# The second normalization's inverse root in a PSUM bank: two dependent steps a round in place of three

## What is computed

```python
x = x + tanh(g_xattn) * xattn(layernorm(x), ctx)      # window attention, 8 heads, 16 keys
x = x + tanh(g_ffn) * ffn(layernorm(x))
def layernorm(x, eps=1e-5):
    return (x - mean(x)) / sqrt(var(x) + eps)         # over the 2048 positions of a channel
def ffn(h):
    logits = einsum('th,eh->te', h, router_weight) + router_bias
    topk_w, topk_idx = top_k(softmax(logits), 8)
    w_dense = zeros.at[tokens, topk_idx].add(topk_w)
    return h * topk_w.sum(-1) + einsum('te,eh->th', w_dense, expert_bias)
```

## Time and profile before

| what | value |
|---|---|
| median of 3 runs | 1548.85 us (1548.09 to 1548.88) |
| profiled execution | 1549.06 us, span in the trace 1547.0 us |
| mean granted TensorE clock | 0.974 of full speed |
| TensorE busy | 1457.9 us (94%) |
| VectorE, ScalarE, GpSimd busy | 1232.8, 1156.2, 1160.6 us |

### The profile page before, as it was taken

How to read it: one execution, slowest core, us unless ns; L and a number is a source line. 1 busy time by engine, 2 the same in 40 slices (tenths; PEclk the granted TensorE clock), 3 DMA queues, 4 the chain that set the end, 5 groups by cost and what they waited for, 6 DMA issues and landing times.

```text
span 1547.0 us, 66674 instructions
## 1 busy us (share of the span) xinstructions
PE 1457.9 (94%) x28162; PEld 1196.4 (77%) x28162; DVE 1232.8 (80%) x2938; ACT 1156.2 (75%) x2025; POOL 1160.6 (75%) x1126
## 2 busy tenths in 40 slices
PE   4799999999999999999999999999999999999986
PEld 3577877878887888888788888878888887778764
DVE  5477887878888787888888788888878888787774
ACT  3588877778787877888787787878778787767652
POOL 4587777788777878778787887878788787677661
PEclk9799999999999999999999999999999999999896
DMA  7454455554545555454555545455554545434232
GB/s 231 122 127 107 127 149 140 145 161 113 162 131 140 144 154 162 112 161 133 140 144 154 162 114 162 131 140 147 152 161 114 160 133 140 123 82 134 57 77 90
DMA packets 365576, 210.39 MB, mean 136 GB/s; under 512 B 294496, under 2 KB 295520, under 8 KB 361056
## 3 DMA queue, kind: packets, MB, share of 16 engines
q1 hardware_dynamic: 365280, 206.14, 49.1%
HBM read 136.88 MB, written 33.55 MB: 110 GB/s over the span
## 4 chain that ended last, share of the span: by engine, by line
PE 60%; DVE 19%; issue 6%; ACT 6%; POOL 5%; DMA 2%; SPq 1%; POOLq 0%; ACTq 0%; DVEq 0%
PE ps_j L1123 26%; PE ps_s L1183 9%; PE ps_a L1148 7%; PE ps_r L1225 6%; PE ps_s L1123 5%; DVE prob_t L908 4%; DVE st_x L915 2%; PE ps_s L1178 2%; POOL prob L495 2%; PE ps_a L1202 2%; PE ps_t L1165 1%; PE ps_a L1203 1%; DMA x_in<-x_dram 1%; DVE st_in L820 1%; DVE nt_x L814 1%
## 5 line engine op out<-in xcount | busy, mean ns | idle before, releaser
L488 POOL TENSOR_TENSOR score<-score,p_inv 128x384 f32<-128x384 f32 x256 | 219.2, 856 | 110.5 <-DVE p_inv L902 107.6
L495 POOL TENSOR_TENSOR prob<-score,prob 128x384 f16<-128x384 f32 x256 | 262.6, 1026 | 32.8 <-ACT prob L660 31.6
L1183 PEld LDWEIGHTS ps_s<-kv_win,q_col 32*32 32x32 f32 x16384 | 197.2, 106 | 59.2 <-issue 58.7
L1183 PE MATMUL ps_s<-kv_win,q_col 32*32 32x48 f32 x16384 | 233.8, 205 | 4.0 <-issue 3.8
L908 DVE STREAM_TRANSPOSE prob_t<-prob 128x512 f32<-128x512 f32 x256 | 177.1, 701 | 68.0 <-POOL prob L495 67.4
L469 POOL TENSOR_TENSOR c_lo<-c_in,c_hi 128x1024 fp32r<-128x1024 f32 x64 | 152.7, 2385 | 91.0 <-ACT c_hi L634 91.0
L1148 PEld LDWEIGHTS ps_a<-prob_t,v_diag 128*128 128x128 f16 x6528 | 175.8, 98 | 51.0 <-DVE prob_t L908 34.0
L1148 PE MATMUL ps_a<-prob_t,v_diag 128*128 128x48 f16 (+2 forms) x6528 | 188.3, 183 | 26.9 <-DVE prob_t L908 20.2
L464 POOL TENSOR_TENSOR att_lo<-att,att_hi 128x512 fp32r<-128x512 f32 x128 | 161.7, 1275 | 50.1 <-ACT att_hi L620 48.8
L598 ACT ACTIVATE kv_win<-ps_j,v_bias 128x512 f16<-128x512 f32 x128 | 108.2, 847 | 104.0 <-PE ps_j L1123 104.0
L1123 PE MATMUL ps_j<-c_hi,wkv_hi 128*128 128x512 f32 x512 | 172.5, 419 | 14.1 <-POOL c_lo L469 7.0
(11 more groups left out here) (149 smaller groups left out, 3320.0 us busy)
## 6 DMA issues: line engine op xcount, KB each, us to landing
v_diag<-v_turn SPq DMA_DIRECT2D x512, 68.0 KB
c_in<-ctx_dram SPq DMA_DIRECT2D x64, 512.0 KB, 4.9
x_in<-x_dram SPq DMA_DIRECT2D x64, 512.0 KB, 5.7
x_res<-x_dram SPq DMA_DIRECT2D x64, 512.0 KB, 4.7
out_dram<-x SPq DMA_DIRECT2D x32, 1024.0 KB, 8.0
c_sq<-ctx_dram SPq DMA_DIRECT2D x60, 512.0 KB, 5.6
x<-ctx_dram SPq DMA_DIRECT2D x4, 512.0 KB, 7.0
x<-experts_dram SPq DMA_DIRECT2D x2, 512.0 KB, 10.2
```

The lines of the kernel that those rows point to most:

```text
L488: pool.tensor_tensor(score[:, u], score[:, u], p_inv[:, u, :].unsqueeze(2).to_broadcast([P, HALF, KEYS]), ALU.mult).then_inc(pm_rdy, 1)
L495: pool.tensor_tensor(part(prob[:, u % 2], 1)[:, :, 0:KEYS], score[:, u], part(prob[:, u % 2], 0)[:, :, 0:KEYS], ALU.subtract).then_inc(pl_ ...
L1183: ins = pe.matmul(s[head(h), n * KEYS:(n + 1) * KEYS], q_col[head(h), g, at:at + SUB], kv_win[c % 2][head(h), 0, g, at:at + KEYS], start=F ...
```

## The change

The tiles `var_x1`, `half_x1` and `nt_x1` move to six columns of the bank `ps_r` (256 to 261), which the router doesn't use. A round becomes two dependent steps: one instruction a group that multiplies `half` by `rs` twice, `rs` once as a per-partition scalar and once as a tensor, and then the instruction that was the third. The two groups' instructions don't wait for one another. A memset at the end, which waits for the last step, reports `ln2_rdy`. Since VectorE now writes to the bank to which TensorE writes the logits, there are two more waits: VectorE's in front of the root for the router's matmuls of the same step, and TensorE's in front of the router of step (b, 1) for `ln2_rdy`.

```diff
-        nt_x1 = sb("nt_x1", [P, G])
-        var_x1 = sb("var_x1", [P, G])
-        half_x1 = sb("half_x1", [P, G])
...
         ps_r = bank("ps_r")
+        SPARE = 2 * P
+        var_x1, half_x1, nt_x1 = [ps_r[:, SPARE + i * G:SPARE + (i + 1) * G] for i in range(3)]
...
+            ROOT2 = 13
+
+            def inverse_root_psum(b):
+
+                base = (b - 1) * ROOT2
+                dve.tensor_scalar(var_x1, mv_x1[:, :, 1], EPS, None, ALU.add).then_inc(root2, 1)
+                dve.tensor_scalar(half_x1, mv_x1[:, :, 1], EPS, -0.5, ALU.add, ALU.mult).then_inc(root2, 1)
+                dve.tensor_scalar(neg_mean_x1[:], mv_x1[:, :, 0], -1.0, None, ALU.mult).then_inc(root2, 1)
+                dve.wait_ge(root2, base + 2)
+                dve.tensor_scalar(rs_x1[:].bitcast(I32), var_x1.bitcast(I32), -0.5, float(RSQRT_SEED),
+                                  ALU.mult, ALU.add).then_inc(root2, 1)
+                for i in range(3):
+                    dve.wait_ge(root2, base + 4 + 3 * i)
+                    for g in range(G):
+                        dve.scalar_tensor_tensor(nt_x1[:, g:g + 1], half_x1[:, g:g + 1], rs_x1[:, g:g + 1],
+                                                 rs_x1[:, g:g + 1], ALU.mult, ALU.mult).then_inc(root2, 1)
+                    dve.wait_ge(root2, base + 6 + 3 * i)
+                    dve.scalar_tensor_tensor(rs_x1[:], nt_x1, 1.5, rs_x1[:], ALU.add, ALU.mult).then_inc(root2, 1)
+                dve.wait_ge(root2, base + ROOT2)
+                dve.memset(pad[:, 3:4], 0.0).then_inc(ln2_rdy, 1)
...
                     need(dve, aggr2, b * (G + 1))
-                    inverse_root(root2, (b - 1) * ROOT, mv_x1, var_x1, half_x1, nt_x1, rs_x1, neg_mean_x1, ln2_rdy)
+                    need(dve, r_mm, nth(b, c, -2))
+                    inverse_root_psum(b)
...
                     ch, _ = place(c, -2)
+                    if c == 1 and seq(b - 1):
+                        need(pe, ln2_rdy, b)
                     need(pe, xt_rdy[1], nth(b, c, -2))
```

## The result

The changed kernel takes 1535.08 us (median of 4 runs, 1531.85 to 1536.9) against 1548.87 us; the ratio is 0.9909, with an interval of 0.9888 to 0.993. It was timed twice more beside the kernel before, with ratios of 0.9923 (0.9893 to 0.9954) and 0.992 (0.99 to 0.994). So it is faster by 12 to 14 us.

What follows compares the result with a forecast made beforehand. TensorE, busy 94%, was taken as the bound, with gains left where it waits. From 1549.06 us, -4.8 - 0.6 - 8.7 - 7.5 + 3.4 = -18.2, and 0.2 to the median, gave 1530.7 us; range 1526 to 1537, without rival (a) 1526 to 1534.

Steps and rivals of the forecast that it cites:

- The stalls go: VectorE's root steps, with at most one SBUF tensor, no longer wait for GpSimd; no step over 0.35 us.
- rival (c): In the root, the SBUF scalar or SBUF tensor still holds a step behind GpSimd; slower, 1554 us; chance 0.05.
- Length of the root: From the root's start to the transposes on VectorE: 2.4 us, against 2.93 before.
- Rival (a): PSUM steps at the upper bound, or TensorE meets another wait: ordinary roots gain nothing; 1536 us; chance 0.13.
- Ordinary roots: TensorE's idle time before attending goes: 0.40 us at each of twelve roots (-4.8), and -0.6 at root 11.
- Roots 14 and 15: Long stalls beside GpSimd's `c_lo` vanish with the low clock behind them: 8.7 us and 7.5 us saved.
- step (14, 2): L1099, held 2.29 us behind GpSimd, stays unchanged; in the range, -3.9 if its stall vanishes, +3.3 if low clock lengthens.
- Rival (b): Stalls go, but at roots 14 and 15 the clock still falls or a wait remains; 1541 us; chance 0.07.
- The tail: Last router, step (16, 1), waits uncovered for the last root: 2.3 us later plus 1.1 for low clock, +3.4.
- VectorE's wait for the router: In front of the root, VectorE waits for router matmuls that ended earlier in the same step: costs nothing.

## Why the prediction came out as it did

**The stalls go: right.** 96 and 48 executions of the new steps lie within 15 ns of each other, 60 of them started beside `prob`; the same arithmetic in SBUF is held as before. That the per-partition scalar in SBUF does not count as a second input, which rival (c) put in doubt, is shown by the 31 of L832 among them. The prediction's evidence was better than the one overlap it named: 58 of its 64 executions of L1047 and L1052 started inside an `x_lo`, and none was over 0.29 us. Here the measurement agrees with the Trainium skill (SBUF — State Buffer, Who interferes with whom) if its two inputs are read as two tensors. What the prediction did not see is that the long stall hung on the short one: it took each root's stalls as separate, but with the 0.7 us beside `prob` gone the changed root is over before `c_lo` begins. Whether a root in SBUF that only avoids `prob` would do as well was not run.

**Length of the root: right, a little long.** 2.29 us measured, 2.4 predicted, against 2.93. The step with the scalar came at 215 to 229 ns (0.215 used), the one without at 159 to 163 (0.21 used): the scalar and not PSUM makes the difference, since the same steps in SBUF take 205 ns at the least and 218 at the median with it, and 160 without. Rival (a) falls.

**Ordinary roots: right.** -4.8 and -0.6 us were predicted. From root 2 to root 14 the kernel before takes 1084.0 us and the changed one 1078.8: 5.2 us less; with roots 14 to 16 in SBUF, the runs say 5.6 (3.3 to 7.9). The idle time behind each of the thirteen is gone.

**Roots 14 and 15: right in kind, too large in size.** This is the term that was mis-sized: 3.67 + 5.05 and 2.43 + 5.05 us, 16.2 together. The periods show what it was worth, in all profiles of this study:

| period | root in SBUF | root in PSUM | mean difference |
|---|---|---|---|
| root 14 to 15 | 100.8, 97.0, 97.7, 98.1 | 92.8, 91.1, 91.1, 95.7, 91.7, 92.7 | 5.9 |
| root 15 to 16 | 83.5, 83.8, 85.6, 84.6, 83.0 | 76.5, 79.3, 78.9, 77.8, 79.2, 76.6, 78.2, 79.1 | 5.9 |

(The first line leaves out the three kernels with the weights in PSUM.) That is 11.8 us in place of 16.2, give or take some 2.5 (twice the standard error of these means); the difference, 4.4 us, is as large as the whole error of the forecast. The runs of the kernel with these two roots alone say 15.0 (12.1 to 18.0), so the size of the miss is not known better than that.

The idle time was right: 3.2 and 3.0 us on average behind roots 14 and 15 in SBUF, 6.2 together, where the prediction had 6.1. The clock's share was not. The time at the granted clock of 0.50 within the same periods, in the same order:

| period | root in SBUF | root in PSUM | mean difference |
|---|---|---|---|
| root 14 to 15 | 13.7, 6.8, 6.8, 10.2 | 3.4, 0, 0, 10.2, 0, 3.4 | 6.5 |
| root 15 to 16 | 17.1 in all five | 6.8, 10.2, 10.7, 10.2, 10.2, 6.8, 10.2, 10.2 | 7.7 |

So 14.2 us of low clock went and not twice 10.1; at half the level that is 7.1 us in place of 10.1. Only a small part of this is that the profile of before was an unlucky one: of the ten stretches behind a held root 14 or 15, seven lasted 10.2 us and three 6.8. The larger part is that the prediction let the stretches go and put nothing in their place, while low clock appeared behind other waits of the same periods. Behind the 3.07 us of idle time that stay some 42 us after root 15 (near 1465) a stretch of 3.4 or 6.8 us came in six of eight profiles with root 15 in PSUM, against two of five with it in SBUF; behind the 2.2 us at step (14, 2) came none, one of 3.4 or one of 10.2. Rival (b) feared a low clock that is not given back, at other waits than these. Why the same idle time is followed by none or by a long one stays open; no run was made to vary it alone. The 6.2 us of idle time and the 7.1 are 13.3, and the periods shrank by 11.8; the other 1.5 us lie within the scatter.

**The tail: right.** +3.4 us were predicted. From the start of the root to the end it is 24.3 us before (1522.64 to 1546.95) and 27.6 after (1505.85 to 1533.41), 3.3 us. The wait alone had 2.7, and so has the mean over all profiles (24.4 against 27.1, from the negated mean). The 2.1 us of waiting are shown; the rest is the clock's, 0.6 us on average in place of the 1.1 predicted, and comes and goes.

**VectorE's wait for the router: nothing, right.** The root starts 0.04 us behind the aggregation, as before.

With the measured sizes the sum is -5.2 - 5.9 - 5.9 + 2.7 = -14.3 us, and 12 to 14 were measured. The first profile of the changed kernel had bad luck besides, two low stretches before root 2, and lies 1.8 us above its median.

**The range: partly luck.** The forecast's own range was 1526 to 1534, for causes of its own (the step (14, 2), a little more or less at each root). 1535.08 lies in the part that was added for rival (a), slow steps or another wait at the ordinary roots, and neither came. The range holds the time for a reason that it did not foresee.

## What to carry to other kernels

A tiny VectorE step with two SBUF tensors can last as long as the GpSimd instruction that it meets; where such steps stand in a chain in front of TensorE, look at their maximum, not at their mean, and give one of the two tensors a place in PSUM. Before sharing a bank with matmuls for that, look at the place where the new wait has no cover, usually the end. If a held step makes a chain late, look for what the chain meets only because it is late. A term that contains the clock should be sized from several profiles, and by the low clock of the whole stretch and not of one wait: a low stretch that goes may come back behind the next wait.

## What the runs showed of the hardware

For VectorE steps of one or two elements, a PSUM operand cost next to nothing: 159 to 163 ns with one PSUM and one SBUF tensor read, 162 to 166 ns for the first conversion written to PSUM against 168 to 172 into SBUF, 168 to 169 ns where PSUM is both read and written, against 160 all in SBUF. The 62 cycles more of the Trainium skill (VectorE: DVE Perf Modes, The TRN2 errata) do not appear there, and the measurement decides. A per-partition scalar cost about 60 ns wherever the tensors lay: 215 to 229 ns in PSUM, 205 at the least and 218 at the median in SBUF. In the router's steps of 128 and more elements it depends on the step: the cast of 128x130 takes 0.28 us from PSUM and 0.22 from SBUF, the subtraction of 128x128 0.29 us with the tensor in PSUM and 0.29 at the least with both in SBUF.
